# A graph network with a gate and an expert layer: the opening and the row normalization of the gate stage rearranged

## The reference, cut to what matters

```
x = x + gnn(layernorm(x));  x = x + ffn(layernorm(x))      # x: 1250 x 1024, float32

def gnn(x, ...):                     # 8 relations, 21250 edges
    u = x @ root + bias + sum over r of mean_r(x[src]) @ weight[r]
    z = concatenate([u, x]) @ w_gate + b_gate              # w_gate: 2048 x 1024
    return tanh(u) * z + x * (1.0 - z)

def ffn(x, ...):                     # 8 experts, the best 2 for each row, H = 256
    softmax of x @ gate_w.T, top 2, SwiGLU of each chosen expert, weighted sum
```

## Time and profile before

| | |
|---|---|
| median of 3 runs | 1788.55 us (1785.87 to 1791.45) |
| the profiled execution, its own time | 1788.47 us |
| its span, first to last instruction | 1786.7 us |
| the gate stage within it | about 1281 to 1459 us from the start |
| TensorE busy, granted clock over the span | 95%, 0.978 |

### The profile page before, as it was taken

The page is one execution under the profiler, slowest core; times in us unless marked ns, Lnnn a source line. Parts: engine busy times, 40 slices in busy tenths (PEclk is TensorE's granted clock), DMA queues, the critical chain, the costliest instruction groups (busy, mean ns, idle before and its releaser), DMA issues. The chain is left out here.

```text
span 1786.7 us, 22169 instructions
## 1 busy us (share of the span) xinstructions
PE 1699.1 (95%) x7876; PEld 1401.9 (78%) x7876; DVE 1096.3 (61%) x1502; ACT 727.5 (41%) x1230; POOL 765.3 (43%) x663
## 2 busy tenths in 40 slices
PE   7999999999999999999999999999799957999996
PEld 6888888888888888888877787877678856787885
DVE  8554666564564343434489999999889977434300
ACT  2315666541331312222266566666522203454453
POOL 1002222215776565601256665555255522555532
PEclk9999999999999999999999999999899977999999
DMA  5336555547224434343598888888844445786653
GB/s 209 95 118 210 187 164 171 181 152 253 88 95 129 142 119 144 112 146 129 196 356 298 286 294 295 290 287 299 276 170 158 149 146 193 191 238 168 179 105 59
DMA packets 140715, 333.94 MB, mean 187 GB/s; under 512 B 19234, under 2 KB 35666, under 8 KB 140608
## 3 DMA queue, kind: packets, MB, share of 16 engines
q0 software_dynamic: 50816, 159.29, 29.5%
q1 hardware_dynamic: 89792, 173.23, 28.9%
HBM read 236.07 MB, written 96.39 MB: 186 GB/s over the span
## 5 line engine op out<-in xcount | busy, mean ns | idle before, releaser
L1275 POOL DMA_INDIRECT gathered<-Y,edge_row x184 | 232.7, 1265 | 179.7 <-PE banks L1444 139.8
L724 ACT ACTIVATE ghi<-gathered,edge_w 128x1024 fp32r<-128x1024 f32 x184 | 211.1, 1151 | 139.1 <-DMA gathered<-Y,edge_row 92.0
L1251 POOL DMA_INDIRECT edge_w<-INV,edge_key x184 | 209.0, 1136 | 119.8 <-DMA edge_w<-INV,edge_key 99.5
L1302 PE MATMUL banks<-whi,xhi 128*128 128x512 f32 x640 | 252.8, 395 | 0.6 <-DVE xlo L911 0.6
L1088 DVE SCALAR_TENSOR_TENSOR glo<-gathered,edge_w,ghi 128x1024 fp32r<-128x1024 f32 x184 | 235.1, 1278 | 24.3 <-ACT ghi L724 24.0
L1304 PE MATMUL banks<-whi,xlo 128*128 128x512 f32 x640 | 249.6, 390 | 0.0
L1303 PE MATMUL banks<-wlo,xhi 128*128 128x512 f32 x640 | 249.6, 390 | 0.0
L1443 PE MATMUL banks<-ghi,sel 128*128 128x512 f32 x368 | 145.4, 395 | 10.0 <-DVE glo L1088 9.5
L674 ACT ACTIVATE ring_hi<-raw_chunk 128x512 fp32r<-128x512 f32 x112 | 66.5, 624 | 207.6 <-PE banks L1406 150.1
L1444 PE MATMUL banks<-glo,sel 128*128 128x512 f32 x368 | 143.4, 390 | 0.0
L1302 PEld LDWEIGHTS banks<-whi,xhi 128*128 128x128 f32 x640 | 120.5, 188 | 25.4 <-DVE xlo L911 1.2
(11 more groups left out here) (332 smaller groups left out, 3678.7 us busy)
## 6 DMA issues: line engine op xcount, KB each, us to landing
raw<-in_L_ffn_w SPq DMA_DIRECT2D x24, 1024.0 KB, 9.1
Y<-y_out SPq DMA_DIRECT2D x80, 256.0 KB, 3.3
t_set<-in_L_gnn_weight POOLq DMA_DIRECT2D x64, 256.0 KB, 4.9
TW<-t_set POOLq DMA_DIRECT2D x64, 256.0 KB, 3.8
raw_chunk<-TW SPq DMA_DIRECT2D x64, 256.0 KB, 2.8
w_stage<-in_L_gnn_weight SPq DMA_DIRECT2D x30, 512.0 KB, 5.0
raw_chunk<-in_L_gnn_weight SPq DMA_DIRECT2D x48, 256.0 KB, 2.9
Y<-half_v SPq DMA_DIRECT2D x40, 256.0 KB, 2.2
```

The source lines that it names most:

```text
L724: nc.scalar.activation(ghi[:, t % HR], gath[t % GR][:], ACT.Copy, scale=edge_w[:, t:t + 1]).then_inc(g_hi, 1)
L1251: nc.gpsimd.indirect_dma_start(out=edge_w[:, t:t + 1], out_offset=None, in_=INV, in_offset=bass.IndirectOffsetOnAxis(ap=edge_key[:, t:t + ...
L1275: nc.gpsimd.indirect_dma_start(out=gath[t % GR][:], out_offset=None, in_=Y, in_offset=bass.IndirectOffsetOnAxis(ap=edge_row[:, t:t + 1], a ...
L1302: pe.matmul(psum[slot][:], xhi[:, k, at], whi[h][:, k], start=(k == 0), stop=False)
```

## The change

TensorE now begins `gate(0, 0)` right after `turn_u(0)`, then turns tile 1, makes `gate(0, 1)`, and only then turns `gw_rows`. The second u buffer moves, so that `fetch_u(1)` is issued with `fetch_u(0)`; the pieces 6 and 7 of `w_gate` are loaded ahead of `xr`, `zg`, the bias and `gw_rows`. ScalarE and VectorE interleave the splits of the weight with the work on tiles 0 and 1. `x_norm` goes from one instruction on VectorE to two on ScalarE: `mean - x`, then times `rstd`, so that `xn` has its sign turned; on ScalarE it stands behind `u_tanh(j+1)` and ahead of `xt_part(j-2)`. GpSimd now adds the bias to `zg` first, and then, for the turned sign, adds where it subtracted and subtracts where it added.

```diff
--- before.py
+++ after.py
@@ -356,14 +356,15 @@
         ulo = za.put("ulo", [P, 2, D], F32R)
         zb.at += 8 * KB
         u = [nc.alloc_sbuf_tensor_at(f"u{i}", [P, D], F32, offset=o)
-             for i, o in enumerate((OFF_YOUT + 4 * KB, OFF_YOUT))]
+             for i, o in enumerate((OFF_YOUT + 4 * KB, OFF_W1 + 16 * KB))]
         xr = zb.put("xr", [P, 2, D], F32)
         zg = zb.put("zg", [P, 2, D], F32)
         th = zb.put("th", [P, 2, D], F32)
         xn = zb.put("xn", [P, 2, D], F32)
         x1 = zc.put("x1", [P, 2, D], F32)
         xn2 = zc.put("xn2", [P, 2, D], F32)
-        xn2t = zc.put("xn2t", [P, KC, P], F32)
+        zc.at += 4 * KB
+        xn2t = nc.alloc_sbuf_tensor_at("xn2t", [P, KC, P], F32, offset=OFF_YOUT)
         bgate_b = zc.put("bgate_b", [P, D], F32)
         gw_rows = zc.put("gw_rows", [P, D], F32)
         gw_t = zd.put("gw_t", [P, KC, X], F32)
@@ -542,6 +543,7 @@
                                 sp.wait_ge(y_out3[i], 16 * NT)
                             sp.wait_ge(g_used, ET - (ET - GR) % GR)
                             fetch_u(0)
+                            fetch_u(1)
                         if g == 3 and j == NT - 1:
                             sp.wait_ge(y_ready3, 4 * NT)
                             load4(2)
@@ -556,18 +558,15 @@
                     if g < 2:
                         load3(g + 2, 0)
                         load3(g + 2, 1)
-                for n in (4, 5):
+                for n in range(4, 8):
                     load4(n)
                 for i in range(2):
                     sp.wait_ge(y_out3[i], 16 * 2 * NT)
-                fetch_u(1)
+                fetch_x(0)
                 sp.wait_ge(g_used, ET)
+                sp.dma_start(bgate_b[:], b_gate.partition_broadcast(P)).then_inc(rows_in, 16)
+                fetch_x(1)
                 sp.dma_start(gw_rows[0:X, :], gate_w).then_inc(small_in, 16)
-                fetch_x(0)
-                sp.dma_start(bgate_b[:], b_gate.partition_broadcast(P)).then_inc(rows_in, 16)
-                for n in (6, 7):
-                    load4(n)
-                fetch_x(1)
                 for j in range(NT + 1):
                     if j + 2 < NT:
                         fetch_u(j + 2)
@@ -747,17 +746,31 @@
                     nc.scalar.activation(wghi[:, 2 * q:2 * q + 2, h * HALF:(h + 1) * HALF], place,
                                          ACT.Copy).then_inc(w_hi4, 1)
 
-                def u_part(j):
+                def u_hi(j):
                     for g in range(2):
                         act.wait_ge(tu_done, 2 * j + g + 1)
                         if j >= 2:
                             act.wait_ge(z_done, 2 * (j - 1))
                         nc.scalar.activation(uhi[:, j % 2, g * BANK:(g + 1) * BANK], psum[g][:],
                                              ACT.Copy).then_inc(uhi_done, 1)
+
+                def u_tanh(j):
                     if j >= 2:
                         act.wait_ge(x1_done, j - 1)
                     act.wait_ge(u_done, j + 1)
                     nc.scalar.activation(th[:, j % 2], u[j % 2][:], ACT.Tanh).then_inc(th_done, 1)
+
+                def x_norm(j):
+                    i = j % 2
+                    act.wait_ge(x_in[i], 16 * (j // 2 + 1))
+                    if j >= 2:
+                        act.wait_ge(sum_done, j - 1)
+                    else:
+                        act.wait_ge(g_used, ET)
+                    nc.scalar.activation(xn[:, i], xr[:, i], ACT.Identity, scale=-1.0,
+                                         bias=mean[:, j:j + 1]).then_inc(xn_done, 1)
+                    act.wait_ge(xn_done, 2 * j + 1)
+                    nc.scalar.activation(xn[:, i], xn[:, i], ACT.Copy, scale=rstd[:, j:j + 1]).then_inc(xn_done, 1)
 
                 def xt_part(j):
                     for g in range(2):
@@ -770,15 +783,28 @@
                 act.wait_ge(y_ready3, 4 * NT)
                 split_hi4(0)
                 split_hi4(1)
-                u_part(0)
-                for n in range(2, 8):
-                    split_hi4(n)
+                u_hi(0)
+                split_hi4(2)
+                split_hi4(3)
+                u_tanh(0)
+                split_hi4(4)
+                split_hi4(5)
+                u_hi(1)
+                split_hi4(6)
+                split_hi4(7)
+                x_norm(0)
+                u_tanh(1)
                 act.wait_ge(gwt_done, 1)
                 nc.scalar.activation(gw_t[:], psum[7][:, 0:KC * X].rearrange("p (k e) -> p k e", e=X),
                                      ACT.Copy).then_inc(gwt_evac, 1)
+                for i in range(2):
+                    act.wait_ge(y_out3[i], 16 * 2 * NT)
                 for j in range(NT):
+                    if 1 <= j < NT - 1:
+                        u_hi(j + 1)
+                        u_tanh(j + 1)
                     if j + 1 < NT:
-                        u_part(j + 1)
+                        x_norm(j + 1)
                     if j >= 2:
                         xt_part(j - 2)
                 xt_part(NT - 2)
@@ -1132,12 +1158,6 @@
                         at = (slice(None), j % 2, slice(g * BANK, (g + 1) * BANK))
                         v.tensor_tensor(ulo[at], psum[g][:], uhi[at].bitcast(F32), ALU.subtract).then_inc(ulo_done, 1)
 
-                def x_norm(j):
-                    i = j % 2
-                    dve.wait_ge(x_in[i], 16 * (j // 2 + 1))
-                    v.tensor_scalar(xn[:, i], xr[:, i], mean[:, j:j + 1], rstd[:, j:j + 1],
-                                    ALU.subtract, ALU.mult).then_inc(xn_done, 1)
-
                 def finish(j):
                     i = j % 2
                     dve.wait_ge(bg_done, j + 1)
@@ -1179,10 +1199,11 @@
                 split_lo4(0)
                 split_lo4(1)
                 u_low(0)
+                split_lo4(2)
+                split_lo4(3)
                 make_u(1)
-                for n in range(2, 8):
+                for n in range(4, 8):
                     split_lo4(n)
-                x_norm(0)
                 for j in range(NT):
                     if j + 1 < NT:
                         u_low(j + 1)
@@ -1190,8 +1211,6 @@
                         finish(j - 1)
                     if j + 2 < NT:
                         make_u(j + 2)
-                    if j + 1 < NT:
-                        x_norm(j + 1)
                 finish(NT - 1)
 
             @block.gpsimd
@@ -1279,12 +1298,12 @@
                 pool.wait_ge(rows_in, 16)
                 for j in range(NT):
                     i = j % 2
-                    pool.wait_ge(xn_done, j + 1)
-                    pool.wait_ge(th_done, j + 1)
-                    nc.gpsimd.tensor_tensor(th[:, i], th[:, i], xn[:, i], ALU.subtract).then_inc(diff_done, 1)
                     pool.wait_ge(g_in4[i], 16 * (j // 2 + 1))
                     nc.gpsimd.tensor_tensor(zg[:, i], zg[:, i], bgate_b[:], ALU.add).then_inc(bg_done, 1)
-                    nc.gpsimd.tensor_tensor(xr[:, i], xr[:, i], xn[:, i], ALU.add).then_inc(sum_done, 1)
+                    pool.wait_ge(xn_done, 2 * j + 2)
+                    pool.wait_ge(th_done, j + 1)
+                    nc.gpsimd.tensor_tensor(th[:, i], th[:, i], xn[:, i], ALU.add).then_inc(diff_done, 1)
+                    nc.gpsimd.tensor_tensor(xr[:, i], xr[:, i], xn[:, i], ALU.subtract).then_inc(sum_done, 1)
 
             @block.tensor
             def _(pe):
@@ -1494,11 +1513,14 @@
 
                 pe.wait_ge(y_evac3, 4 * NT)
                 turn_u(0)
+                gate(0, 0)
+                turn_u(1)
+                gate(0, 1)
                 pe.wait_ge(small_in, 16)
                 for k in range(KC):
                     ins = pe.transpose(psum[7][:, k * X:(k + 1) * X], gw_rows[0:X, k * P:(k + 1) * P], ident[0:X, 0:X])
                 ins.then_inc(gwt_done, 1)
-                for j in range(NT):
+                for j in range(1, NT):
                     if j + 1 < NT:
                         turn_u(j + 1)
                     gate(j, 0)
```

## The result

The changed kernel takes 1803.89 us in the median of 6 runs (1799.68 to 1812.25), the kernel before 1787.53 (1783.16 to 1791.45, 6 runs): the ratio is 1.0093, with a 95% interval from 1.0077 to 1.0109. It is slower, by 16.4 us, where 21.7 were forecast. The profiled execution of the change is its slowest, 1812.25 us with a span of 1810.5; a second profile, of an execution of 1801.78 us, comes among the experiments and matters for what follows.

A forecast was written before the change was run, and what follows sets the result against it. A ring of engines, not TensorE's 14.4 us of work, was taken to set the gate stage's 15.6 us step. Opening -3.8, steps +19.2 and end +6.3 gave +21.7 on 1788.47: 1810 us, range 1794 to 1818.

The forecast's parts named there:

- The queue: ScalarE's `x_norm` waits for `xr`, delaying `xt_part`, logits, turn and `uhi`; `u_low` starts 5 to 7 us later in a step.
- No table load: ScalarE's Identity passes in the gate stage need no table load; otherwise two more a step, +2.6 us.
- x1 freed from GpSimd: VectorE's x1 no longer collides with GpSimd's passes and falls from 3.29 to 1.23 us.
- The clock, and with it the step: Nearly all logits and turns on TensorE run at the lower clock: 18.8 us a step, +19.2 us over steps 3 to 8.
- Rival A: Same ScalarE queue, but TensorE's clock stays high: 16.9 us a step, +8.3 us in all, 1797 us; chance 20%.
- The opening: Stage start: earlier first gate product makes x1 of step 2 end 3.8 us sooner; bounds 7.5 us or nothing.
- The end: The last gate pair waits for the late `logits(6)` and ends 24.4 us after x1 of step 8, not 18.1: +6.3 us.
- Rival C: Gate stage: freed VectorE leaves TensorE as the bound at 14.4 us a step, -11.0 us, 1777.5 us; chance 8%.

The follow-up runs named there:

- the opening alone: Changed kernel with `x_norm` back on VectorE and GpSimd's passes in their old order and signs: 1786.01 us, 0.9994 of the kernel before.
- 6 matmuls more: Changed kernel with 6 extra matmuls into an unread bank ahead of each logits: 1802.91 us, 1.009 of the kernel before.
- the kernel with one pass: Changed kernel without `x_norm`'s second pass, the product with `rstd`: 1797.05 us, 1.0053 of the kernel before.
- 6 or 12 matmuls more: Changed kernel with 6 or 12 extra matmuls into an unread bank ahead of each logits: 1802.91 us with 6, 1803.64 us with 12.
- the kernel with four buffers: Changed kernel with two more `xr` buffers, `xr` asked for two tiles sooner and `zg` issued first: 1778.68 us, 0.9953 of the kernel before.

## Why the prediction was right

**The queue: right.** `xt_part` behind the wait for `xr`, logits behind `xt_part`, turn, `uhi` and `u_low` behind logits: the profile after shows each link, and turning the two calls takes the loss away. `xr` was in at T + 5.4 to 6.2 (5.4 forecast), the two passes took 2.24 us up to `xt_part` (2.3). No table load came with Identity: the trace has one in the stage, as before. The Trainium skill's page that the prediction names for this ("ScalarE: Activation LUTs", section "Table sets: the hidden batching unit") agrees. 1.15 us for a pass with one operand per row against 1.06 without: the Trainium skill ("ScalarE: Activation LUTs", section "What ACT_TABLE_LOAD costs") gives some 0.09 us for such an operand, and the trace agrees.

**x1 freed from GpSimd: right.** 1.22 us for 3.29, and the freed time was more than spent.

**The clock, and with it the step: mis-sized.** "I take nearly all of logits and the turn at the lower level: 18.8 us a step." In the slowest execution it was 18.55; in one near the median 17.37, with one step of six at the lower level in its logits. The idle time ahead of logits was put at over 2 us; in five of the six steps of the second profile it was 0.4 to 1.1. I took what TensorE's 14.4 us leave of a step, and left out that a fall of the clock makes that work longer and the idle time shorter. Rival A (16.9 a step, 1797 us) was about as near to the median as the forecast, 7 us below it and 6 above. In its steps it was nearer: five of the six in the second profile average 16.96.

**The opening: mis-sized.** -3.8 forecast, -1.0 measured, in the opening alone and in the whole change. All that follows is counted from the start of `turn_u(0)` (1283.44 before, 1285.42 after). The first gate product came at 3.4 us, as forecast. The first gate then took 8.3 us, not 7.6, and turn 2 began 2.0 us sooner than before (21.3 against 23.3 us), forecast 2.7. The gain was to grow by 1.1 us after that, and it shrank by 1.0. Turn 2 stands at the same time in both traces, 1306.75 before and 1306.76 after, and `uhi` of that tile comes 0.9 us later after it. The first row is of before:

```profile
1307.39 1.09 ACT L755 ACTIVATE uhi<-banks 128x512 fp32r<-128x512 f32 x2 [5.39 <-PE banks L1461]
...
1306.09 1.15 ACT L770 ACTIVATE xn<-xr,mean 128x1024 f32<-128x1024 f32 x1
1307.27 1.15 ACT L773 ACTIVATE xn<-xn,rstd 128x1024 f32<-128x1024 f32 x1
1308.33 1.07 ACT L754 ACTIVATE uhi<-banks 128x512 fp32r<-128x512 f32 x2
```

`uhi` stands behind `x_norm(1)`, and that behind the copy of the turned `gw_rows`, which TensorE now makes later. The prediction had this as "about 0.2 us". VectorE's product then begins 1.3 us sooner than before and not 2.0, and one step later `uhi` is behind `x_norm` again. That VectorE's product and x1 are held by GpSimd (3.32 and 3.30 us) is no part of the difference: it is so before (3.27 and 3.30). In the opening alone there is no `x_norm` on ScalarE, and its -1.0 has another path: there the one on VectorE is held to 2.87 us behind turn 2, and `u_low` waits for it.

The bias rows, first needed by GpSimd, landed only 9.6 us after their issue. This did not delay GpSimd's next pass, since after the pass with the bias it waited another 1.90 us for `xn`.

**The end: right.** logits(7) at T(8) + 24.4 forecast; 24.5 in the second profile (1460.42 less 1435.92), 26.0 in the slowest execution, 18.1 before.

The sum from the second profile: -1.1 + 6 x (17.37 - 15.6) + 6.4 = +15.9, against 16.4 in the medians. That execution itself is only 13.3 us above the profiled one of before, since what follows the stage took 2.2 us less in it. Beside the forecast's -3.8 + 19.2 + 6.3, the steps were put 8.6 us too high, and the gain of the opening 2.7 us too large. The two errors partly cancel: that the forecast came within 5.8 us of this sum is in part luck.

**Rival C.** Its mechanism, a ring freed until TensorE's 14.4 us bound the step, did not come with the change, for the reason the prediction gave: `xn` waits for `xr`. With `xr` early and `zg` first it nearly did, 14.65 us a step.

## What to carry to other kernels

An engine with idle time is no free place for work: ask what the moved instruction waits for, and what stands behind it in that queue. A wait that was hidden on one engine, because it came late to it, is bare on an engine that comes early; load the operand sooner (here two more buffers, -0.5% against before) rather than move the instruction. Where two engines hold each other up, find which pass meets which before reordering: here 1 us in the landing of `zg` decided whether a step took 14.7 or 15.6 us.

## What the runs showed of the hardware that was not expected

The same program's steps took 16.7 to 20 us, mostly by where the clock fell: in the second profile logits ran at the lower level after 4.6 us without work (3.58 us) and at the high one after 0.4 to 1.1 us (1.95), and the fall came afterwards, in the gate's matmuls. In the slowest execution they ran at the lower level after 2.25 us without work too (3.56). The idle time just before does not settle it alone: with 6 matmuls more, logits after 2.97 us without work took 1.95 us, and in the kernel with one pass they took 1.95 us after 1.46 and 2.55 us after 1.52. With 6 or 12 matmuls more, logits took 1.8 to 2.2 us in steps 3 to 8, and nothing was gained in the median.

A VectorE instruction need not be large to be held: 128x1 with two inputs took 2.41 us beside GpSimd's passes and 0.22 alone. Nor need it have two large inputs: `x_norm`, with one input of 128x1024 and two of one number per row, took 2.85 us held and 0.81 alone.

Two transfers of 512 KB issued 0.5 us apart do not land together. In the changed kernel `xr` landed a median of 5.0 us after its issue and `zg`, behind it, 5.8 us after its own. In the kernel with four buffers `zg`, in front, landed after 4.8 us, and put behind `xr` again after 5.4.
